# Batched LayerNorm statistics and an integer-seeded Newton root in the output-projection stage of a scan and ternary-weight FFN layer

## What is computed

```
x = x + layernorm(attn(layernorm(x)))          # per row of 1024, eps 1e-5
x = x + layernorm(ffn(layernorm(x)))

attn(u): delta = softplus(u @ Wd.T + bd)
         state[e, n] = exp(-delta*a_pos)*state + delta*b*u     # scan over T = 2048, n = 16
         y = state.sum(n);  return y @ Wo.T + bo
ffn(u):  gate = silu(bitlinear(u, w_gate)); up = bitlinear(u, w_up)
         return bitlinear(gate*up, w_down)                     # inner size 4096
bitlinear: activations rounded to 127 levels of the row's maximum, weights to -1, 0, 1 times a scale
layernorm(x) = (x - mean) / sqrt(var + eps)
```

## Time and profile before

| what | us |
|---|---|
| device time, median of 2 runs | 4028.19 (4027.37 to 4029.0) |
| device time of the profiled execution | 4032.09 |
| span of its slowest core (core 4), first to last instruction | 4030.3 |
| spans of the 8 cores | 3994.7 to 4030.3 |
| TensorE matmuls busy | 1309.1 (32%) |
| VectorE busy | 1497.9 (37%) |
| ScalarE busy | 1453.5 (36%) |
| GpSimd busy | 267.2 (7%) |

### The profile page before, as it was taken

How to read it: one execution, slowest core, us unless ns; L and a number is a source line. 1 busy time by engine, 2 the same in 40 slices (tenths; PEclk the granted TensorE clock), 3 DMA queues, 4 the chain that set the end, 5 groups by cost and what they waited for, 6 DMA issues and landing times.

```text
span 4030.3 us, 25581 instructions; the slowest of 8 cores (3994.7 to 4030.3 us)
## 1 busy us (share of the span) xinstructions
PE 1309.1 (32%) x5260; PEld 537.3 (13%) x5260; DVE 1497.9 (37%) x2016; ACT 1453.5 (36%) x2110; POOL 267.2 (7%) x443
## 2 busy tenths in 40 slices
PE   1121111200011111212743621743633725528453
PEld 0000000100000000000311200311211312103221
DVE  0005656479800000100266982267412477021500
ACT  2653544333344444356323343323123223132201
POOL 0001212123300000000010220000000000000000
PEclk9965555655555555655875655875666866658666
DMA  4042222100022222123410101310110301113111
GB/s 67 0 167 94 73 84 84 21 11 0 16 94 94 94 94 94 47 63 125 136 63 11 52 12 42 95 63 11 52 52 24 103 30 37 42 37 107 50 47 47
DMA packets 164346, 245.36 MB, mean 61 GB/s; under 512 B 6113, under 2 KB 121058, under 8 KB 160098
## 3 DMA queue, kind: packets, MB, share of 16 engines
q1 hardware_dynamic: 159906, 235.07, 17.6%
q0 software_dynamic: 4288, 8.65, 1.4%
HBM read 218.80 MB, written 33.55 MB: 63 GB/s over the span
## 4 chain that ended last, share of the span: by engine, by line
DVE 24%; PE 23%; ACT 21%; DMA 14%; issue 10%; POOL 5%; ACTq 1%; DVEq 1%; SPq 0%; POOLq 0%
DVE s_sig L289 10%; PE pD L995 7%; POOL s_state L263 5%; PE pG L868 4%; PE pU L876 4%; DMA s_td<-tdT 4%; DVE s_sig L296 4%; DMA wu_b<-wu 3%; DMA wg_b<-wg 3%; DVE s_ytmp L313 2%; PE ptD L954 2%; ACT s_h L961 2%; PE pW L682 2%; DVE s_qs L903 2%; DMA wdn_b<-wdn 2%
## 5 line engine op out<-in xcount | busy, mean ns | idle before, releaser
L282 ACT ACTIVATE s_abar<-s_dyq,s_nega 128x512 f32<-128x512 bf16 x512 | 369.4, 722 | 632.1 <-DVE s_sig L289 487.0
L289 DVE TENSOR_TENSOR_SCAN s_sig<-s_abar,s_state,s_lnf 128x512 bf16<-128x512 f32 x384 | 492.9, 1284 | 103.7 <-ACT s_abar L282 64.1
L995 PE MATMUL pD<-s_td,s_h 128*128 128x512 bf16 x1024 | 392.1, 568 | 220.9 <-DMA s_td<-tdT 217.3
L868 PE MATMUL pG<-s_tg,s_dyq 128*128 128x512 bf16 x1024 | 397.9, 389 | 105.3 <-DVE s_h L898 84.2
L876 PE MATMUL pU<-s_tu,s_dyq 128*128 128x512 bf16 x1024 | 397.2, 388 | 0.0
L263 POOL TENSOR_TENSOR s_state<-s_sig,s_onesp 128x1 bf16<-128x1 bf16 x384 | 248.7, 648 | 1678.5 <-ACT s_abar L282 898.5
L313 DVE SCALAR_TENSOR_TENSOR s_ytmp<-s_sig,s_bprm,s_ytmp 128x512 bf16<-128x512 bf16 x448 | 336.5, 751 | 48.2 <-DVE s_sig L289 1.4
L898 DVE TENSOR_TENSOR s_h<-s_gtmp,pU 128x512 bf16<-128x512 bf16 x128 | 88.0, 688 | 533.4 <-ACT s_gtmp L890 533.4
L688 DVE TENSOR_TENSOR attnC<-pW,s_borep 128x512 f32<-128x512 f32 x16 | 11.1, 692 | 586.8 <-PE pW L682 586.5
L890 ACT ACTIVATE s_gtmp<-pG,s_r1g 128x512 bf16<-128x512 f32 x128 | 88.0, 687 | 340.4 <-PE pU L876 188.2
L995 PEld LDWEIGHTS pD<-s_td,s_h 128*128 128x128 bf16 x1024 | 135.4, 136 | 476.7 <-issue 462.7
(11 more groups left out here) (155 smaller groups left out, 1706.6 us busy)
## 6 DMA issues: line engine op xcount, KB each, us to landing
wg_b<-wg SPq DMA_DIRECT2D x32, 1024.0 KB, 5.7
wu_b<-wu SPq DMA_DIRECT2D x32, 1024.0 KB, 5.6
wdn_b<-wdn SPq DMA_DIRECT2D x32, 1024.0 KB, 5.5
s_tg<-tgT SPq DMA_DIRECT2D x64, 512.0 KB, 3.8
s_tu<-tuT SPq DMA_DIRECT2D x64, 512.0 KB, 4.8
s_td<-tdT SPq DMA_DIRECT2D x64, 512.0 KB, 3.7
tgT<-wg_stage SPq DMA_DIRECT2D x16, 512.0 KB, 3.4
tuT<-wu_stage SPq DMA_DIRECT2D x16, 512.0 KB, 3.4
```

What stands on the lines that cost most here:

```text
L282: lambda h, d=dc, n_=n, p=pa: h.activation(out=s_abar[:, p, :], in_=delta_view[:, d, t0:t0 + QT], func=AF.Exp, scale=s_nega[:, d, n_:n_ + 1]),
L289: lambda h, d=dc, c_=col, p=pa, s=ps: h.tensor_tensor_scan(s_sig[:, s, :], s_abar[:, p, :], lnT_view[:, d, t0:t0 + QT], s_state[:, c_:c_ + 1],
L868: h.matmul(pGs[c_][:], q1T_view[:, k, t_ * 128:(t_ + 1) * 128], s_tg[:, wp, k4_, :], start=(k == 0), stop=(k == KC - 1)),
L995: lambda h, c_=c, k=kc, p=par, s_=sub, f=hf: h.matmul(pDs[c_][:, f * 512:(f + 1) * 512], q2T_view[:, c_, k, :], s_td[:, p, s_, f * 512:(f ...
```

## The change

emit_C_q takes the statistics of its four tiles together, in both passes. attnC becomes attnC4, four bf16 slices of 1024 columns, one for each tile, where it was one f32 row of 1024 columns; ln3C is an f32 view of the first two slices. In the first pass a first loop runs matmuls, bias and the two sums for each tile; then emit_newton4 makes the four inverse roots and shifts on VectorE from the sums in sC_st; a second loop normalises each tile and adds the residual. In the second pass a first loop takes the sums of the four tiles, emit_newton4 follows, and the second loop does the rest tile by tile as before, injected steps included. Ln and Exp are no longer used in this stage. emit_newton4 has the same 20 operations as the kernel already has at L1025 to L1061. The first LayerNorm still uses emit_lnstats.

```diff
+        sC_st = S("sC_st", [128, 8], F32)
+        sC_nt = S("sC_nt", [128, 16], F32)
...
+        def emit_newton4(st4, nt, t_sums):
+            sch.add("vector", lambda h: h.tensor_scalar(
+                nt[:, 0:4], st4[:, 0:4], 1.0 / D, None, ALU.mult),
+                waits=[t_sums, sch.chain("vector")])
...
+            sch.add("vector", lambda h: h.tensor_scalar(
+                iy, iy, -1, 0x5F3759DF, ALU.mult, ALU.add),
+                waits=[sch.chain("vector")])
...
+            return ST("vector")
...
         def emit_C_q(q, w_first=(), inject=None):
             tcs = range(4 * q, 4 * q + 4)
-            with nc.sbuf_tensor(f"attnC{q}", [128, D], F32) as attnC, \
+            with nc.sbuf_tensor(f"attnC{q}", [128, 4, D], BF16) as attnC4, \
...
-                ln3C = attnC
+                ln3C = attnC4[:, 0:2, :].bitcast(F32).rearrange("p a b -> p (a b)")
...
-                    for tc in tcs:
+                    for ci, tc in enumerate(tcs):
...
-                        sch.add("vector", lambda h: h.tensor_tensor(attnC[:, 0:512], pW0[:],
-                                                                    s_borep[:, 0:512], ALU.add),
-                                waits=[t_mm, ("dma_borep", 16), sch.chain("vector")])
+                        sch.add("vector", lambda h, c_=ci: h.tensor_tensor(
+                            attnC4[:, c_, 0:512], pW0[:], s_borep[:, 0:512], ALU.add),
+                            waits=[t_mm, ("dma_borep", 16), sch.chain("vector")])
...
                         t_attn = ST("vector")
-                        t_st = emit_lnstats(attnC[:], lnscC, waits=[t_attn])
-                        sch.add("scalar", lambda h: h.activation(out=lnscC[:], in_=attnC[:],
-                                                                 func=AF.Identity,
-                                                                 scale=s_stats[:, 4:5],
-                                                                 bias=s_stats[:, 5:6]),
-                                waits=[t_st], inc=1)
+                        sch.add("scalar", lambda h, c_=ci: h.activation(
+                            out=lnscC[:], in_=attnC4[:, c_, :], func=AF.Identity,
+                            accum_out=sC_st[:, c_:c_ + 1]),
+                            waits=[t_attn, sch.chain("scalar")])
+                        sch.add("scalar", lambda h, c_=ci: h.activation(
+                            out=lnscC[:], in_=attnC4[:, c_, :], func=AF.Square,
+                            accum_out=sC_st[:, 4 + c_:5 + c_]),
+                            waits=[sch.chain("scalar")])
+                    t_rs2 = emit_newton4(sC_st, sC_nt, ST("scalar"))
+                    for ci, tc in enumerate(tcs):
+                        sch.add("scalar", lambda h, c_=ci: h.activation(
+                            out=lnscC[:], in_=attnC4[:, c_, :], func=AF.Identity,
+                            scale=sC_nt[:, 8 + c_:9 + c_], bias=sC_nt[:, c_:c_ + 1]),
+                            waits=([t_rs2] if ci == 0 else []) + [sch.chain("scalar")])
                         t_ln2 = ST("scalar")
                         sch.add("vector", lambda h, t_=tc: h.tensor_tensor(
                             s_x1[:, t_, :], s_x1[:, t_, :], lnscC[:], ALU.add),
...
                 with nc.psum_tensor(f"ptC{q}", [128, 4, 1024], BF16) as ptC:
-                    for tc in tcs:
-                        t_st3 = emit_lnstats(s_x1[:, tc, :], lnscC)
+                    for ci, tc in enumerate(tcs):
...
+                    t_rs3 = emit_newton4(sC_st, sC_nt, ST("scalar"))
+                    for ci, tc in enumerate(tcs):
                         sch.add("scalar",
-                                lambda h, t_=tc: h.activation(out=ln3C[:], in_=s_x1[:, t_, :],
-                                                              func=AF.Identity,
-                                                              scale=s_stats[:, 4:5],
-                                                              bias=s_stats[:, 5:6]),
-                                waits=[t_st3], inc=1)
+                                lambda h, t_=tc, c_=ci: h.activation(
+                                    out=ln3C, in_=s_x1[:, t_, :], func=AF.Identity,
+                                    scale=sC_nt[:, 8 + c_:9 + c_], bias=sC_nt[:, c_:c_ + 1]),
+                                waits=([t_rs3] if ci == 0 else []) + [sch.chain("scalar")])
                         t_ln3 = ST("scalar")
```

More of the change, by code:

```diff
@@ L517, in build_nc @@
                                       [(d_wdn, d_tdT, D, DI, 4, "wdn")])
+        def emit_newton4(st4, nt, t_sums):
+            sch.add("vector", lambda h: h.tensor_scalar(
+                nt[:, 0:4], st4[:, 0:4], 1.0 / D, None, ALU.mult),
+                waits=[t_sums, sch.chain("vector")])
+            sch.add("vector", lambda h: h.tensor_tensor(
+                nt[:, 4:8], st4[:, 0:4], nt[:, 0:4], ALU.mult),
+                waits=[sch.chain("vector")])
+            sch.add("vector", lambda h: h.tensor_tensor(
+                nt[:, 4:8], st4[:, 4:8], nt[:, 4:8], ALU.subtract),
+                waits=[sch.chain("vector")])
+            sch.add("vector", lambda h: h.tensor_scalar(
+                nt[:, 4:8], nt[:, 4:8], 1.0 / D, EPS, ALU.mult, ALU.add),
+                waits=[sch.chain("vector")])
+            iv = nt[:, 4:8].bitcast(I32)
+            iy = nt[:, 8:12].bitcast(I32)
+            sch.add("vector", lambda h: h.tensor_scalar(
+                iy, iv, 1, None, ALU.logical_shift_right),
+                waits=[sch.chain("vector")])
+            sch.add("vector", lambda h: h.tensor_scalar(
+                iy, iy, -1, 0x5F3759DF, ALU.mult, ALU.add),
+                waits=[sch.chain("vector")])
+            for _ in range(3):
+                sch.add("vector", lambda h: h.tensor_tensor(
+                    nt[:, 12:16], nt[:, 8:12], nt[:, 8:12], ALU.mult),
+                    waits=[sch.chain("vector")])
+                sch.add("vector", lambda h: h.tensor_tensor(
+                    nt[:, 12:16], nt[:, 12:16], nt[:, 4:8], ALU.mult),
+                    waits=[sch.chain("vector")])
+                sch.add("vector", lambda h: h.tensor_scalar(
+                    nt[:, 12:16], nt[:, 12:16], -0.5, 1.5, ALU.mult, ALU.add),
+                    waits=[sch.chain("vector")])
+                sch.add("vector", lambda h: h.tensor_tensor(
+                    nt[:, 8:12], nt[:, 8:12], nt[:, 12:16], ALU.mult),
+                    waits=[sch.chain("vector")])
+            sch.add("vector", lambda h: h.tensor_tensor(
+                nt[:, 0:4], nt[:, 0:4], nt[:, 8:12], ALU.mult),
+                waits=[sch.chain("vector")])
+            sch.add("vector", lambda h: h.tensor_scalar(
+                nt[:, 0:4], nt[:, 0:4], -1.0, None, ALU.mult),
+                waits=[sch.chain("vector")])
+            return ST("vector")
@@ L687, in emit_C_q @@
                         t_mm = ST("tensor")
-                        sch.add("vector", lambda h: h.tensor_tensor(attnC[:, 0:512], pW0[:],
-                                                                    s_borep[:, 0:512], ALU.add),
-                                waits=[t_mm, ("dma_borep", 16), sch.chain("vector")])
-                        sch.add("vector", lambda h: h.tensor_tensor(attnC[:, 512:1024], pW1[:],
-                                                                    s_borep[:, 512:1024], ALU.add),
-                                waits=[sch.chain("vector")])
@@ new lines, in emit_C_q @@
+                        sch.add("vector", lambda h, c_=ci: h.tensor_tensor(
+                            attnC4[:, c_, 512:1024], pW1[:], s_borep[:, 512:1024], ALU.add),
+                            waits=[sch.chain("vector")])
+                        t_attn = ST("vector")
+                        sch.add("scalar", lambda h, c_=ci: h.activation(
+                            out=lnscC[:], in_=attnC4[:, c_, :], func=AF.Identity,
+                            accum_out=sC_st[:, c_:c_ + 1]),
+                            waits=[t_attn, sch.chain("scalar")])
@@ L707, in emit_C_q @@
                 with nc.psum_tensor(f"ptC{q}", [128, 4, 1024], BF16) as ptC:
-                    for tc in tcs:
-                        t_st3 = emit_lnstats(s_x1[:, tc, :], lnscC)
-                        sch.add("scalar",
-                                lambda h, t_=tc: h.activation(out=ln3C[:], in_=s_x1[:, t_, :],
-                                                              func=AF.Identity,
-                                                              scale=s_stats[:, 4:5],
-                                                              bias=s_stats[:, 5:6]),
-                                waits=[t_st3], inc=1)
+                    for ci, tc in enumerate(tcs):
+                        sch.add("scalar", lambda h, t_=tc, c_=ci: h.activation(
+                            out=lnscC[:], in_=s_x1[:, t_, :], func=AF.Identity,
+                            accum_out=sC_st[:, c_:c_ + 1]),
```

(12 more changed lines are left out.)

## The result

| | before | after |
|---|---|---|
| device time, median | 4028.19 us (4024.45 to 4033.72, 6 runs) | 3982.23 us (3977.39 to 3989.01, 7 runs) |
| profiled execution: device time | 4032.09 | 3986.58 |
| profiled execution: span of the slowest core | 4030.3 | 3984.9 |
| spans of the 8 cores | 3994.7 to 4030.3 | 3954.6 to 3984.9 |

The ratio is 0.9885, with a 95% interval of 0.9873 to 0.9897: 46 us less, where 67 were forecast.

A forecast was written before the change was run, and what follows sets the result against it. No engine was taken as the bound: the kernel is a serial string of stages. First passes 59.8 us less plus second passes 7.6 make 67.4 less, so 3961 on the median's scale, against 4028.19 before; range 3948 to 3985.

The forecast's parts named there:

- First pass, overlap and clock: emit_C_q's first pass: matmuls overlap the previous tile's sums, a risen clock stays; periods 5.50, first 8.10 for q = 1 to 3.
- rival 1: First passes: the clock falls in each pause between bursts, periods 8.1, time 3984 (3994 if never high); chance 0.15.
- granted clock: TensorE's granted clock in the first passes of the profile after: above 0.68.
- First pass, tail: Behind the first pass's last matmul bias: sums, Newton batch, four serial normalisations with adds, 20.51 us per pass.
- Second pass: emit_C_q's second pass: sums and Newton taken once for four tiles, 1.9 us less each, 7.6 for four.
- Costs taken as nothing: Taken as free: bf16 attnC, table loads, SP's queue order, number of accumulating instructions.
- stages outside emit_C_q that change by over 5 us: Listed among signs in the profile after that the prediction was wrong: untouched stages changing by over 5 us.
- A microsecond taken out of emit_C_q should therefore come off the end: Nothing overlaps with emit_C_q, so time saved there shortens the whole kernel; 67.4 us in sum.
- the forecast itself: Whole kernel's time near 3961, taken as 3950 to 3972 us, chance 0.71.
- Rival 2: Part of the gain isn't passed on, for instance the q = 0 stage gives nothing: 3980; chance 0.06.
- Rivals 3 and 4: 3: luckier down-projection bursts, 3947, chance 0.06; 4: gate and up stage loses the higher clock, up to 4109, chance 0.02.

The follow-up runs named there:

- e1: Changed kernel with sC_st and sC_nt moved out of the persistent tensors into one 512-byte tensor inside emit_C_q: 3968.53 us, ratio 0.983 to before.
- e8: e1 with two buffers for normalised rows, second pass's sums moved into the first's tail, second pass working on two tiles at a time: 3899.49 us, ratio 0.9676.
- e2: Kernel before with one unused tensor of 96 bytes a partition ahead of s_w: 4058.46 us, ratio 1.0045.
- e3: Kernel before with 64 unused bytes a partition ahead of s_w: 4054.12 us, ratio 1.0039.
- e6: Kernel before with 128 unused bytes a partition ahead of s_w: 4049.68 us, ratio 1.0048.
- e4: Kernel before with one wait changed: next tile's matmuls wait for L691, not VectorE's newest instruction; statistics stay per tile: 3964.9 us, ratio 0.982.
- e5: Kernel before with only the f32 rings that wg and wu are loaded into starting 96 bytes later: 4029.96 us, ratio 1.0.
- e9: Kernel before with 96 unused bytes ahead of wg_stage (same for wu), so only the stores' source tile moves: 4041.07 us, ratio 1.0031.
- e12: Kernel before with 256 unused bytes a partition ahead of s_w: 4030.39 us, ratio 1.0001.
- e11: Kernel before with 512 unused bytes a partition ahead of s_w: 4025.94 us, ratio 0.9995.
- e10: Kernel before with the ternary tile of wg and wu 96 bytes further on and the stage 512 bytes further on: 4028.16 us, ratio 1.0001.

## Why the prediction was right, and where 20 us went

**First pass, overlap and clock: held.** Forecast a period of 5.50 and bursts of 3.62 after an idle of 1.9; measured 5.49, 3.61 and 1.88. In 29 of the 32 first passes (8 cores, 4 each) the clock, once at the 2.4 GHz level, stayed there. For q = 1 to 3 the first period was forecast at 8.10; on core 4 it was 8.44, 7.92 and 7.86. The exceptions are q = 2 on core 4, below, q = 2 on core 5 (43.3 us in all, bursts of 5.68 and 4.36) and the last burst of q = 0 on core 6 (4.36):

```profile
2977.62 6.05 PE L726 MATMUL pW<-s_w,s_dyq 128*128 128x512 bf16 x16 [31.31 <-DVE attnC L735]
...
2985.55 5.62 PE L726 MATMUL pW<-s_w,s_dyq 128*128 128x512 bf16 x16 [1.88 <-DVE attnC L735]
...
2993.05 4.36 PE L726 MATMUL pW<-s_w,s_dyq 128*128 128x512 bf16 x16 [1.88 <-DVE attnC L735]
```

The bursts of 5.62 and 4.36 were partly at 1.2 GHz, after the same idle of 1.88. In e1 and e8, with the same periods of 5.49, none of 144 such bursts fell. The Trainium skill's section that I weighed in the prediction ("TensorE: Matmul & The Clock Gate", section "A second HAM failure mode: psum-queue depth-cycling") tells of such swings as a frequent thing; the traces agree in 5 bursts of 216 (after, e1 and e8 together). So rival 1 happens now and then and costs 0.7 to 3 us where it does; in the first passes without it, 37.3 (q = 0) and 39.1 to 40.6, it did not. What decides it isn't shown. The granted clock, forecast above 0.68, was 0.75, 0.67, 0.62 and 0.72: two of the four are below, since the first burst behind the long idle is mostly at 1.2 GHz and weighs more in a stretch that has become shorter, and in q = 2 two more bursts were partly slow.

**First pass, tail: small by 0.3 to 0.6 us a pass.** From the last L732 to the first L749 the forecast was 1.58 + 2.50 + 5.51 = 9.59, measured 9.66 (q = 0 and 3) and 10.01 (q = 1 and 2); each of the four normalisations with its add takes 2.78 instead of 2.73. That is 1.9 us over the four passes. They are 160.3 on core 4, 4.4 above the forecast's 155.8, and the rest of these 4.4 are the slower bursts of q = 2. On average over the cores they are 158.5: a gain of 56.8 instead of 59.8.

**Second pass: held.** 52.4 on core 4 at q = 2, 52.3 on average over q = 1 to 3 and the cores, 52.2 forecast. bf16 attnC cost nothing:

```profile
L732 DVE TENSOR_TENSOR attnC<-pW,s_borep 128x512 bf16<-128x512 f32 x16 | 11.1, 692 | 587.5 <-PE pW L726 587.2
```

692 ns for the bias with bf16 result, as the earlier trace rows suggested. The 20 table loads stayed 20.

**"Costs taken as nothing": here the working had a hole.** The list has data types, table loads, queue order and accumulations, and lacks what two new persistent tensors do to everything allocated behind them. It costs 16.8 us in the preparation, and for q = 0 most likely also the 3 to 4 us by which the stretch with the preparation of wdn misses the forecast (+1.8 where -1.9 was expected). That stretch is 265.6 in e1, 273.0, 271.4 and 270.2 with the unused bytes of e2, e3 and e6, and 269.5 and 268.0 in e4 and e5 on the same chips; single cores differ by up to 10 us in it, so this points to the placement and doesn't show it. For wg and wu it is shown by e1, e2, e3, e6 and e9 to e12; for wdn's own stage no run was made that moves it alone. 67.4 less 16.8, 3.0 and 3.7 is 43.9; 46.0 were measured, and 47.2 on average of the spans, where the gate and up stages and what follows them give another 3.4.

The prediction did give the sign by which one would know ("stages outside emit_C_q that change by over 5 us"), and that is how it was found. Its sentence "A microsecond taken out of emit_C_q should therefore come off the end" held too: e1 took 67.4 forecast and 68.8 measured.

**Where the time fell.** The forecast was 3961, with 3950 to 3972 for the forecast itself, and 3982 is outside of that. It lies inside the full range because that reached up to 3985 for rivals 1 and 2, and what used this room was neither of them but a cost that the working didn't have. So the time came out inside by luck; what the working had right are the terms of emit_C_q.

**Rivals.** Rival 2 (the gain of q = 0 not passed on) gave 3980, within 2 us of what was measured, and was still wrong: q = 0's first pass fell by 16.0 us on average, 16.6 forecast. The time alone would have confirmed it; only the table by stages told them apart. Rivals 3 and 4 had nothing to explain: gate, up and down projections, last LayerNorm and output changed by 3.4 us in all.

## What to carry to other kernels

A new tensor, however small, moves whatever is allocated behind it. Where a transfer reads such a tile in short runs (512 bytes here), keep its start on a multiple of 256 bytes: put small tensors in a scope of their own, as in e1, or fill them up, as e11 and e12 show. Compare the lengths of all stages and not only of the one that was edited.

Where engines take turns, look first at what the next tile really waits for. "Everything given to VectorE so far" instead of the one operation that matters cost 72 us here, and a single wait gives them back; two buffers in place of one, with the order of the operations fitted to them, gave another 60.

## What the runs showed of the hardware

- A store of 512 KB in runs of 512 bytes, from an SBUF tile that starts 64, 96 or 128 bytes behind a multiple of 256, has its last packet done 3.05 us behind its issue instead of 2.62, and the 1 MB load issued 0.46 us behind it lands 0.7 us later (6.2 instead of 5.5, e9 against e10). Starts that are multiples of 256 or 512 show no difference (e10, e11, e12). The load's own destination, written in pieces of 4096 bytes, started 96 bytes off without a price (e5).
- Sixteen matmuls of 512 columns after an idle of 1.88 us took 3.61 us, all at 2.4 GHz, in 211 of 216 cases (after, e1, e8), and 4.36 to 5.68 in the other five, all of them in after: the same idle can go either way.
